# Splitting eight experts' weights one in each of the first eight groups of a token stage, in place of one in every two of sixteen

## What is computed

```python
emb = word_emb[input_ids] + pos_emb
g_j = relu(mean(adj_j @ word_emb[gv_ids_j], axis=1) @ W_j.T + b_j)   # three graphs j
h = layernorm(concat(emb, g_0, g_1, g_2) @ W_proj.T + b_proj)        # stage one
h = h + fft_conv(layernorm(h), k) + layernorm(h) * bias              # a long convolution in time
x = layernorm(h)                                                     # router: top 2 of 8 experts
h = h + sum over the token's two experts of w_e * (gelu(x @ Wi_e.T + bi_e) @ Wo_e.T + bo_e)
```

## Time and profile before

| | us |
|---|---|
| median of 3 runs | 989.66 (989.16 to 992.24) |
| the profiled execution, its span | 995.9 |
| TensorE, VectorE, ScalarE, GpSimd busy | 869.3, 656.0, 536.0, 644.7 |

### The profile page before, as it was taken

One profiled execution on the slowest core, in us unless ns is written; L12 is line 12 of the kernel. 1 busy time (PEld: TensorE's weight loads), 2 busy tenths in 40 slices (PEclk: granted clock), 3 DMA queues, 4 the chain that ended last, 5 costly groups with the idle time before them and its releaser, 6 DMA issues.

```text
span 995.9 us, 22850 instructions
## 1 busy us (share of the span) xinstructions
PE 869.3 (87%) x7469; PEld 822.9 (83%) x7469; DVE 656.0 (66%) x2142; ACT 536.0 (54%) x1271; POOL 644.7 (65%) x552
## 2 busy tenths in 40 slices
PE   3959898998898739893889999999999999999993
PEld 2959898998898738892679999999999989898993
DVE  3167857776867565978756776666667656666662
ACT  1222223213312325599667777777777767677761
POOL 6777777777777300100067886777778768788886
PEclk9957556556756669996699999999999999999997
DMA  8437547457465429855946446745744543343454
GB/s 245 131 87 248 179 153 257 136 200 225 157 207 195 126 86 282 225 166 131 245 101 149 61 60 158 191 61 122 199 83 63 130 96 61 59 60 59 61 57 44
DMA packets 99788, 138.31 MB, mean 139 GB/s; under 512 B 13427, under 2 KB 81430, under 8 KB 97654
## 3 DMA queue, kind: packets, MB, share of 16 engines
q0 software_dynamic: 39552, 53.26, 28.1%
q1 hardware_dynamic: 59142, 73.59, 24.3%
q10 hardware_dynamic: 1008, 10.34, 2.8%
HBM read 98.14 MB, written 39.02 MB: 138 GB/s over the span
## 4 chain that ended last, share of the span: by engine, by line
PE 29%; DMA 22%; POOL 22%; issue 12%; DVE 8%; ACT 4%; DVEq 2%; SPq 1%; POOLq 0%; ACTq 0%
DMA out<-Hs,id_s 20%; POOL ev_g L521 13%; POOL emb_g L512 5%; PE bank L799 3%; PE bank L801 3%; PE bank L800 3%; POOL blob L537 3%; PE bank L780 2%; PE bank L781 2%; PE bank L784 2%; PE bank L783 2%; PE bank L782 2%; DVE hstats L1157 2%; ACT adj_s L956 1%; PE bank L763 1%
## 5 line engine op out<-in xcount | busy, mean ns | idle before, releaser
L975 ACT ACTIVATE Hs<-bank,U 128x256 bf16<-128x256 f32 x426 | 214.0, 502 | 126.0 <-PE bank L784 126.0
L551 POOL DMA_INDIRECT out<-Hs,id_s x142 | 233.5, 1645 | 65.6 <-issue 45.6
L537 POOL DMA_INDIRECT blob<-xtab_d,id_g x142 | 151.6, 1068 | 122.7 <-DVEq L1340 79.6
L521 POOL DMA_INDIRECT ev_g<-in_word_emb,ids_i x192 | 189.7, 988 | 58.5 <-issue 57.9
L976 ACT ACTIVATE Hs<-bank,U 128x256 f32<-128x256 f32 x426 | 216.4, 508 | 0.0
L799 PE MATMUL bank<-U,Hs 128*128 128x192 bf16 x852 | 210.0, 246 | 0.3 <-issue 0.3
L801 PE MATMUL bank<-U,Hs 128*128 128x192 bf16 x852 | 208.8, 245 | 0.0
L800 PE MATMUL bank<-U,Hs 128*128 128x192 bf16 x852 | 208.5, 245 | 0.0
L1362 DVE TENSOR_TENSOR Hs<-Hs 128x512 bf16<-128x512 f32 x213 | 146.8, 691 | 92.1 <-ACT Hs L976 92.0
L780 PE MATMUL bank<-wst,U 128*128 128x256 bf16 x426 | 116.6, 274 | 1.3 <-DVE wst L1351 1.3
L781 PE MATMUL bank<-wst,U 128*128 128x256 bf16 x426 | 116.7, 274 | 0.0
(11 more groups left out here) (216 smaller groups left out, 1643.2 us busy)
## 6 DMA issues: line engine op xcount, KB each, us to landing
adj_s<-in_adj SPq DMA_DIRECT2D x48, 256.0 KB, 7.3
ev_g<-kpad_d SPq DMA_DIRECT2D x24, 512.0 KB, 5.8
U<-blob_d SPq DMA_DIRECT2D x14, 771.0 KB, 5.0
wst<-in_wsrc SPq DMA_DIRECT2D x8, 1344.0 KB
blob_d<-blob ACTq DMA_DIRECT2D x7, 1443.0 KB
U<-blob_d SPq DMA_DIRECT2D x14, 672.0 KB, 5.7
xtab_d<-U SPq DMA_DIRECT2D x4, 1552.0 KB, 17.0
out<-Hs SPq DMA_DIRECT2D x4, 1536.0 KB, 12.8
```

The lines of the kernel that those rows point to most:

```text
L521: pool.indirect_dma_start(ev_g[:, p, j, b, :], None, t["word_emb"], bass.IndirectOffsetOnAxis(ap=ids_i[:, 1 + j, i * Q + b:i * Q + b + 1], ...
L537: pool.indirect_dma_start(xg_f[:, q % RX, h, :], None, xtab_d, bass.IndirectOffsetOnAxis(ap=id_g[:, 2 * q + h:2 * q + h + 1], axis=0)).the ...
L551: pool.indirect_dma_start(out, bass.IndirectOffsetOnAxis(ap=id_s[:, 2 * q + h:2 * q + h + 1], axis=0), yo[:, q % RY, h, :], None, compute_ ...
L975: f(hh[w][:, d, :], ps, ACT.Gelu, bias=bi[:, d:d + 1])
```

## The change

The eight experts have their turn in groups 0 to 7, one in each. In group i ScalarE does `split_hi(i)` after `normal(i - 1)` (in group 0 after `graphs(0)`) and issues the store of expert i - 1 between `column_copy(i + 1)` and `graphs(i)`; the store of expert 7 follows group 7, on ScalarE's queue like the others. VectorE does `split_lo(n)` after `rows(n)`, in group 0 ahead of the filter's second argument. SP waits for the store of expert n and loads expert n + 1 after each group's adjacency loads, up to expert 7; the later adjacency loads follow without it. From group 8 on the three engines' loops hold no weights.

```diff
             load_expert(0)
-            with sp.Fori(0, NQ // 2 - 1) as it:
+            with sp.Fori(0, E // 2 - 1) as it:
                 for p in range(2):
 
                     sp.wait_ge(colsum, 2 * it + p + 1)
                     load_adj(2 * it + p + 2, p)
-                sp.wait_ge(w_out, 16 * (it + 1))
-                sp.sem_inc(sp_turn, 1)
-                load_expert(it + 1)
+                    sp.wait_ge(w_out, 16 * (2 * it + p + 1))
+                    sp.sem_inc(sp_turn, 1)
+                    load_expert(2 * it + p + 1)
+            sp.wait_ge(colsum, E - 1)
+            load_adj(E, 0)
+            sp.wait_ge(w_out, 16 * (E - 1))
+            sp.sem_inc(sp_turn, 1)
+            load_expert(E - 1)
+            sp.wait_ge(colsum, E)
+            load_adj(E + 1, 1)
+            with sp.Fori(E // 2, NQ // 2 - 1) as it:
+                for p in range(2):
+                    sp.wait_ge(colsum, 2 * it + p + 1)
+                    load_adj(2 * it + p + 2, p)
...
                 load_toep(s, s)
-            store_expert(sp, E - 1)
...
-            def pairs(it):
+            def pairs(it, prepared):
                 for p in range(2):
                     i = 2 * it + p
                     embedding_copy(i, p)
                     if not (isinstance(i, int) and i == NQ - 1):
                         column_copy(i + 1, 1 - p)
+                    if not (prepared or isinstance(i, int) and i == 0):
+                        store_expert(act, i - 1)
                     graphs(i, p)
                     if isinstance(i, int) and i == 0:
+                        split_hi(0)
                         filter_decay()
                         filter_sine(1)
-                    if p:
-                        split_hi(it)
                     if not (isinstance(i, int) and i == 0):
                         normal(i - 1, 1 - p)
-                if not (isinstance(it, int) and it > 0):
-                    store_expert(act, it)
+                    if not (prepared or isinstance(i, int) and i == 0):
+                        split_hi(i)
 
             column_copy(0, 0)
-            steps(act, NQ // 2, pairs, last=1)
+            pairs(0, False)
+            with act.Fori(1, E // 2) as it:
+                pairs(it, False)
+            store_expert(act, E - 1)
+            with act.Fori(E // 2, NQ // 2 - 1) as it:
+                pairs(it, True)
+            pairs(NQ // 2 - 1, True)
...
-            def pairs(it):
+            def pairs(it, prepared):
+                if not (prepared or isinstance(it, int) and it == 0):
+                    split_lo(2 * it - 1)
                 if not (isinstance(it, int) and it == NQ // 2 - 1):
                     row_sums(2 * it + 2, 0, it + 2)
                 rows(2 * it, 0)
                 if isinstance(it, int) and it == 0:
+                    split_lo(0)
                     filter_argument(1)
                     filter_taps()
-                if not (isinstance(it, int) and it > 0):
-                    split_lo(it)
+                if not (prepared or isinstance(it, int) and it == 0):
+                    split_lo(2 * it)
                 if not (isinstance(it, int) and it == NQ // 2 - 1):
                     row_sums(2 * it + 3, 1, it + 2)
                 rows(2 * it + 1, 1)
 
-            steps(dve, NQ // 2, pairs, last=1)
+            pairs(0, False)
+            with dve.Fori(1, E // 2) as it:
+                pairs(it, False)
             split_lo(E - 1)
+            with dve.Fori(E // 2, NQ // 2 - 1) as it:
+                pairs(it, True)
+            pairs(NQ // 2 - 1, True)
```

## The result

The median went from 990.95 us (four runs, 989.16 to 997.79) to **1094.14 us** (four runs, 1088.71 to 1096.03): slower by a ratio of 1.1018, 95% interval 1.0979 to 1.1056. The forecast was 1095, in a range of 1068 to 1116.

What follows compares the result with a forecast made beforehand. GpSimd's gathers, 20.7 us a group, were taken to pace stage one, TensorE close behind. Rows(15) +108.4 and the end -2.7 sum to +105.7: profiled 995.9 becomes 1101.6, median 1095, range 1068 to 1116.

Steps and rivals of the forecast that it cites:

- Rows(1) at 84.6: VectorE's rows of group 1 were to begin at 84.6 us, after expert 0's split, store, load burst and row sums.
- The ring of 35.1: Groups 1 to 7: rows, split, hand-over, store, load burst through SP's queue and row sums take 35.1 us a group.
- The burst: SP's expert load and then adjacency loads, from issue until landed; taken at 10.7 us in each turn of the ring.
- The bound of 8.4 by the store's rate: Lower bound for the burst: 2112 KB at the store's 250 KB a us would take 8.4 us.
- 28.0 from rows(7) to rows(8): Last split and store ahead of ScalarE's embedding copy for group 8; rows(8) come 28.0 us after rows(7), at 323.3.
- 19.2 a group after that: From rows(8) to rows(15), the ring gone, TensorE paces the groups at 19.2 us each.
- 2.7 given back at the end: Convolution's start: expert 7's store no longer holds SP's Toeplitz loads from the fifth on; -2.7 us.
- GpSimd has slack for the stretched gathers, the copies are covered: Gathers beside splits are stretched within GpSimd's slack; ScalarE's copies are covered by VectorE's rows; no cost, 19 us if uncovered.
- ScalarE's ring alone: Rival: adjacency in time, rows wait for split, store issue, graph features and projection; 26.9 us a group, 1038; chance 0.05.
- A faster burst: Rival: the burst at the store's rate, 8.4 in place of 10.7, seven times; 16 less, 1079; chance 0.17.
- A slower one: Rival: bursts of 12.30 (11 more) and a second half at 20.7 a group (10 more); 1117; chance 0.13.
- Not slower: Rival: adj(n+2) waits last for column sums, not the store, so no ring; gathers stay at 20.7, 988; chance 0.03.

Runs made afterwards that it cites:

- tail_only: Kernel before, with only the store of expert 7 moved behind all Toeplitz loads on SP's queue; 991.25 us, ratio 0.997 to the kernel before.
- adj_ahead: Kernel after, with SP's adjacency loads of group n + 2 ahead of the wait for expert n - 1's store and expert n's load; 1033.3 us, ratio 1.046.
- small_load: Kernel after, with the loads of experts 1 to 7 bringing only 64 of 2688 columns; 1068.53 us, ratio 1.082 to the kernel before.
- store_behind: Kernel after, with the store of expert i - 1 issued behind graphs(i) on ScalarE's queue in groups 1 to 7; 1098.95 us, ratio 1.112.
- both_ahead: Kernel after, with the edits of adj_ahead and store_behind together; 1006.88 us, ratio 1.019 to the kernel before.

## Why the prediction was right

The mechanism is the one that was forecast, and each step has its row now. That 1095 and 1094.14 agree to 1 us is partly luck: rows(8) came 3.9 us later than forecast and the groups behind it took 7.3 us less, so that the stage lost 102.0 us up to the ninth chunk, not 105.7; and four runs of either kernel spread over 7 to 9 us.

- *Rows(1) at 84.6.* Measured 83.6. The store was issued at 65.26, not at 66.7, ahead of the two copies that stand before it on ScalarE's queue (they ran from 65.49 on). So that a queue runs in its written order did not mean, here, that a transfer waits for the copies ahead of it to end.
- *The ring of 35.1.* Measured (299.19 - 83.63) / 6 = 35.9. The burst, taken at 10.7 for having fewer adjacency loads behind it and fewer gathers beside it, was 11.2 in the mean of the seven turns, as long as the six of before (11.3 in the mean, 10.85 to 12.30): neither reason showed. The remaining 0.3 is spread over rows, hand-over and store. The bound of 8.4 by the store's rate was never near. By the formula of the Trainium skill ("DMA: Bandwidth & Descriptors", "Anatomy of one DMA"), a fit for single transfers that GpSimd issues, the burst would be an estimated 7.0; the traces of this burst, several transfers that SP issues with gathers beside them, have 4 us more.
- *28.0 from rows(7) to rows(8).* Measured 327.22 - 299.19 = 28.03.
- *19.2 a group after that.* Measured (454.53 - 327.22) / 7 = 18.2. This is the term that was most off, 7 us over the second half. The 19.2 were read from four groups with splits, in which TensorE waited 2.3 us for row sums and was idle for 2.1 us a group in all. In the second half of the kernel after no wait of TensorE for row sums or gathers shows, and it was idle for 1.2 us a group; its busy time is nearly the same, 17.1 and 17.0 a group. It worked against the ring's 5 us, so that rows(15) was forecast at 457.9 and came at 454.5.
- *2.7 given back at the end.* 37.16 from rows(15) to the ninth chunk before, 34.21 after: 2.95. tail_only shows that the store's place alone does it.
- *GpSimd has slack for the stretched gathers, the copies are covered.* Gathers beside a split were stretched (the one at 170.66 took 2.46 us, against a median of 0.95), but the gathers wait 96.5 us for TensorE, nearly all in the first half, so that the stretch costs nothing. ScalarE's copies began at 151.49 and ended at 154.03 in the turn shown, 16.5 before VectorE's split: covered.
- *The rivals.* ScalarE's ring alone was put at 1038 in a kernel where SP's did not exist; adj_ahead is that kernel, at 1033.3. A faster burst came only with the expert's bytes left out (7.6 us in the mean in small_load, 1068.53). A slower one did not come either: 11.2 us in place of 12.30, and a second half at 18.2 a group in place of 20.7, at a mean granted clock of 0.62 against 0.64 before. Not slower needed the column sums, not the store, to be what adj(n+2) waits for last; SP stood for the stores in seven waits, 241.8 us in all, and no run came near 988 with SP's order as it is.
- *The range.* Its ends, 1068 and 1116, are called the bounds of the burst, but the rivals' own sums give 1079 and 1106 (7 x 1.6 = 11 more) for the burst alone, so it was wider than that reason. And the kernel before is told from no change less sharply than the 0.3% that the prediction gives: its four runs spread over 0.9%.

## What to carry to other kernels

When work is moved to come twice as often, look for the ring that it closes and add up its steps in the order of the queues: here it was 36 us long, harmless while it went round once in 41 us and the bound once it had to go round in 21. An in-order issuing queue ties together what has no data in common; a prefetch that the next step needs goes ahead of a wait that it doesn't. And two rings may lie one under the other: undoing the shorter one's wait shows nothing until the longer one is open (store_behind 1098.95; adj_ahead 1033.3, with both 1006.88).

## What was not expected of the hardware

TensorE's groups in the second half, the same instructions each time and no wait over 0.9 us among them, come in lengths that go with the granted clock. Sums over the groups 8 to 13 (us, busy by engine, granted clock, DMA share, GB/s):

```profile
327.20:345.90 18.70, 17.50 (x92) 17.25 (x91) 12.82 (x55) 4.23 (x10) 10.53 (x12) 0.61 0.33 99
345.90:362.50 16.60, 15.39 (x92) 15.22 (x91) 13.11 (x56) 4.23 (x10) 12.63 (x14) 0.69 0.43 126
362.50:381.90 19.40, 18.20 (x92) 17.92 (x91) 13.12 (x56) 4.24 (x10) 14.55 (x15) 0.58 0.39 117
381.90:400.50 18.60, 17.39 (x92) 17.17 (x91) 13.13 (x55) 4.24 (x10) 14.32 (x15) 0.61 0.44 130
400.50:417.10 16.60, 15.39 (x93) 15.23 (x91) 12.94 (x55) 4.23 (x10) 12.64 (x14) 0.69 0.27 75
417.10:436.60 19.50, 18.29 (x92) 18.02 (x91) 11.34 (x54) 4.22 (x10) 12.83 (x14) 0.58 0.27 75
```

A group takes 16.6 us at a mean granted clock of 0.69, 18.6 or 18.7 at 0.61 and 19.4 or 19.5 at 0.58, means between the two levels of 1.2 and 2.4 GHz; in these six groups the three lengths come round twice in the same order. In adj_ahead, store_behind and small_load the rows of these groups come in the same three steps, 16.6, 18.5 to 18.6 and 19.5; in both_ahead they do not. What sets the turn was not tried. The part behind the convolution, equal in all kernels, differed by 6.8 us between two profiled executions (580.6 and 573.8), nearly as much as the runs of the kernel before spread (989.16 to 997.79): a sum against one profiled execution has that much uncertainty in a part that no edit touches.
